# Other PSUM banks for a late group, a merge moved to the end, and five unread matmuls in a spectral-mixing kernel

## The reference

```python
xf = jnp.fft.rfft2(x, axes=(1, 2), norm='ortho')
o1r = relu(xr @ w1[0] - xi @ w1[1] + b1[0])
o1i = relu(xi @ w1[0] + xr @ w1[1] + b1[1])
o2r = softshrink(o1r @ w2[0] - o1i @ w2[1] + b2[0], 0.01)
o2i = softshrink(o1i @ w2[0] + o1r @ w2[1] + b2[1], 0.01)
out = jnp.fft.irfft2(o2r + 1j * o2i, s=(H, W), norm='ortho') + x
```

## Time and profile before

| what | value |
|---|---|
| median of 3 runs | 5476.74 us (5476.72 to 5477.54) |
| the profiled execution's own time | 5478.67 us |
| its span, first to last instruction | 5475.4 us |
| PE busy, share of the span | 97% |
| DVE busy | 67% |
| ACT busy | 41% |
| mean granted TensorE clock | 0.993 |

### The profile page before, as it was taken

How to read it: one execution, slowest core, us unless ns; L and a number is a source line. 1 busy time by engine, 2 the same in 40 slices (tenths; PEclk the granted TensorE clock), 3 DMA queues, 4 the chain that set the end, 5 groups by cost and what they waited for, 6 DMA issues and landing times.

```text
span 5475.4 us, 112300 instructions
## 1 busy us (share of the span) xinstructions
PE 5302.9 (97%) x44352; PEld 4309.3 (79%) x44352; DVE 3684.5 (67%) x5859; ACT 2217.8 (41%) x3457; POOL 627.1 (11%) x420
## 2 busy tenths in 40 slices
PE   6999999999999999999999999999999999999998
PEld 5777887778777787777877777787778877787777
DVE  5676676676666766767667676676666766766665
ACT  3443434434344343444433443334434344343442
POOL 0110011110111101111011110011100111101111
PEclk9999999999999999999999999999999999999999
DMA  3331333312333113331133321333312333123311
GB/s 101 94 84 29 84 94 94 96 30 70 94 94 98 44 54 94 94 98 48 51 94 94 98 65 35 92 94 98 79 38 75 94 98 94 37 62 94 98 48 47
DMA packets 1065693, 421.12 MB, mean 77 GB/s; under 512 B 1062816, under 2 KB 1062944, under 8 KB 1065120
## 3 DMA queue, kind: packets, MB, share of 16 engines
q1 hardware_dynamic: 1060384, 411.62, 28.2%
q10 hardware_dynamic: 4736, 1.60, 0.1%
HBM read 210.26 MB, written 201.33 MB: 75 GB/s over the span
## 4 chain that ended last, share of the span: by engine, by line
issue 89%; POOL 11%; POOLq 0%; DVE 0%
POOL x L774 11%; POOLq L773 0%; POOLq L777 0%; DVE x L726 0%; POOLq L774 0%; POOLq L786 0%
## 5 line engine op out<-in xcount | busy, mean ns | idle before, releaser
L774 POOL TENSOR_TENSOR x<-shrink_or_v,x 128x480 f32<-128x480 f32 (+1 forms) x416 | 626.9, 1507 | 4840.6 <-DVE shrink_or_v L719 4800.9
L691 DVE TENSOR_TENSOR shrink_or_v<-ps,wts 128x768 f32<-128x768 f32 (+1 forms) x544 | 502.0, 923 | 993.1 <-PE ps L478 993.1
L478 PE MATMUL ps<-wts,hbig 128*128 128x192 f32 x4160 | 821.6, 340 | 0.0
L399 PE MATMUL ps<-tab,ring_h 128*128 128x128 f32 x6144 | 726.7, 283 | 46.2 <-DVE ring_h L745 46.2
L399 PEld LDWEIGHTS ps<-tab,ring_h 128*128 128x128 f32 x6144 | 720.6, 199 | 55.6 <-DVE ring_h L745 55.6
L478 PEld LDWEIGHTS ps<-wts,hbig 128*128 128x128 f32 x4160 | 661.0, 189 | 122.2 <-issue 122.2
L572 ACT COPY zbig<-ps 128x512 f32<-128x512 f32 (+1 forms) x544 | 309.1, 568 | 966.5 <-PE ps L415 966.5
L580 ACT ACTIVATE hsmall<-ps,wts 128x256 f32<-128x256 f32 (+1 forms) x544 | 254.6, 468 | 1084.8 <-PE ps L451 1084.8
L386 PE MATMUL ps<-tab,ring_a 128*64 128x128 f32 x6144 | 680.5, 273 | 3.8 <-ACT ring_a L541 3.8
L387 PE MATMUL ps<-tab,ring_a 128*63 128x128 f32 x6144 | 680.4, 273 | 0.0
L386 PEld LDWEIGHTS ps<-tab,ring_a 128*64 128x64 f32 x6144 | 671.3, 137 | 8.3 <-ACT ring_a L541 4.7
(11 more groups left out here) (52 smaller groups left out, 6620.3 us busy)
## 6 DMA issues: line engine op xcount, KB each, us to landing
x<-in_x SPq DMA_DIRECT2D x128, 1536.0 KB, 12.4
out<-x SPq DMA_DIRECT2D x352, 480.0 KB, 4.8
out<-x SPq DMA_DIRECT2D x32, 432.0 KB, 4.1
wts<-in_mix SPq DMA_DIRECT2D x16, 513.0 KB, 3.6
out<-x SPq DMA_DIRECT2D x32, 240.0 KB, 4.2
out<-x SPq DMA_DIRECT2D x32, 192.0 KB, 4.3
ydg<-row ACTq DMA_DIRECT2D x32, 48.0 KB
yedge<-row ACTq DMA_DIRECT2D x32, 0.8 KB
```

Source lines behind the costliest of these rows:

```text
L399: mm = pe.matmul(ps[:, line_bank(1, g), j * 128:(j + 1) * 128], ring_h[g % RING_H][:, j, :], mat("inv_h"), start=True, stop=True)
L478: mm = pe.matmul(o, hbig[u % 2][:, k * H:(k + 1) * H], mix_part("w2_big"), start=False, stop=True, skip_group_check=True)
L691: dve.tensor_tensor(parts(v), d, b2, ALU.add).then_inc(bias_done, 1)
L774: pool.tensor_tensor(xs[p][:, a:b, :], ucopy[g % 4][:, 0:b - a, :], mirror(xs[p], a, b), ALU.add).then_inc(plus_ready, 1)
```

## The change

1. The second layer of group 15 goes to banks 0 and 1 and no longer to 5 and 6. It waits until ACT and DVE have copied the last transforms out of banks 0 and 1 (`zbig_ready`, `zsmall_ready`) and no longer until DVE has added the bias of group 14.
2. Group 16's second layer goes to bank 5 and waits for the bias of group 14. The merge goes to bank 7.
3. `merge` stands behind the second layer of group 16.
4. Five matmuls of 128 x 128 x 128, which nothing reads, are written to bank 6: two where the merge stood and three behind it (`keep_warm`).
5. ACT packs the first tile before the relu of group 16 and the second right behind it (`early_pack`). Then follow the copy of the merged edges and the other four tiles. Each `early_pack` waits for `shrunk` of group 14.

```diff
-        ZBIG_BANK, ZSMALL_BANK, BIG_BANK, SMALL_BANK, OUT_BANK, LAST_BANK = 0, 1, 2, 4, 5, 7
-        E_BANK = ZSMALL_BANK
+        ZBIG_BANK, ZSMALL_BANK, BIG_BANK, SMALL_BANK, OUT_BANK, E_BANK = 0, 1, 2, 4, 5, 7
...
+        def out_banks(u):
+            bank = ZBIG_BANK if u == NU - 2 else OUT_BANK
+            return slice(bank, bank + 2)
...
                 def mix2_rows(q, u):
                     pe.wait_ge(hid_ready, NU * q + u + 1)
-                    if 0 < u < NU - 1:
-                        pe.wait_ge(bias_done, NU * q + u)
+                    if u == NU - 2:
+                        pe.wait_ge(zbig_ready, NU * (q + 1))
+                        pe.wait_ge(zsmall_ready, NU * (q + 1))
+                    elif u:
+                        pe.wait_ge(bias_done, NU * q + min(u, NU - 2))
...
+                def keep_warm(q, n):
+                    pe.wait_ge(bias_done, NU * q + NU - 2)
+                    for i in range(n):
+                        pe.matmul(ps[:, OUT_BANK + 1, 0:H], mat("inv_h"), mat("fwd_h"), start=True, stop=True)
...
                         mix1_rows(q, NU - 1)
-                        merge(q)
+                        keep_warm(q, 2)
                         mix2_rows(q, NU - 1)
                         mix2_whole(q, NU - 1)
+                        merge(q)
+                        keep_warm(q, 3)
                         inverse_lines(q)
...
+                def early_pack(q, g):
+                    act.wait_ge(shrunk, NU * q + NU - 2)
+                    act.copy(*pack_moves(g, LATE, 128)).then_inc(packed_act, 1)
...
+                            if it == NU:
+                                early_pack(q, 0)
                             if it >= 1:
                                 relu(q, it - 1)
...
+                        early_pack(q, 1)
                         act.wait_ge(merge_done, q + 1)
                         act.copy(ydg[:, 0:2, :].rearrange("p k c -> p (k c)"),
                                  ps[:, E_BANK, 0:2 * CB]).then_inc(merged, 1)
-                        act.wait_ge(shrunk, NU * q + NU - 2)
-                        for g in range(RING_H):
-                            act.copy(*pack_moves(g, LATE, 128)).then_inc(packed_act, 1)
+                        for g in range(2, RING_H):
+                            early_pack(q, g)
```

More of the change, by code:

```diff
@@ L306, in big_cols, with out_bank @@
             return (len(evens(u)) + len(odds(u))) * H
-        def out_bank(u):
-            return LAST_BANK if u == NU - 1 else OUT_BANK
+        def out_banks(u):
+            bank = ZBIG_BANK if u == NU - 2 else OUT_BANK
+            return slice(bank, bank + 2)
+        def out_bank(u, i):
+            return range(8)[out_banks(u)][i]
         def small_rows(u):
@@ L469, in mix2_rows @@
                             half = slice(i * SMALL, (i + 1) * SMALL)
-                            pe.matmul(ps[:, out_bank(u) + i, k * 2 * CB:(k + 1) * 2 * CB],
+                            pe.matmul(ps[:, out_bank(u, i), k * 2 * CB:(k + 1) * 2 * CB],
                                       hsmall[u % 2][half, k * H:(k + 1) * H],
@@ L476, in mix2_whole @@
                     for k in range(n + len(odds(u))):
-                        o = ps[:, out_bank(u) + k // n, k % n * 2 * CB:(k % n + 1) * 2 * CB]
+                        o = ps[:, out_bank(u, k // n), k % n * 2 * CB:(k % n + 1) * 2 * CB]
                         mm = pe.matmul(o, hbig[u % 2][:, k * H:(k + 1) * H], mix_part("w2_big"),
@@ L682, in parts @@
                         return t.rearrange("p (i k c) -> p i k c", i=halves, c=2 * CB)
-                    d = ps[:, out_bank(u):out_bank(u) + halves, 0:ne * 2 * CB].rearrange("p i (k c) -> p i k c", c=2 * CB)
+                    d = ps[:, out_banks(u), 0:ne * 2 * CB][:, 0:halves].rearrange("p i (k c) -> p i k c", c=2 * CB)
                     b2 = mix_part("b2").rearrange("p (i k c) -> p i k c", i=1, k=1).broadcast_to([128, halves, ne, 2 * CB])
```

## The result

| | before | changed |
|---|---|---|
| median | 5476.73 us (5473.81 to 5477.54, 4 runs) | 5402.85 us (5402.58 to 5403.81, 4 runs) |
| profiled execution, its own time | 5478.67 us | 5402.93 us |
| span | 5475.4 us | 5400.7 us |
| mean granted clock | 0.993 | 0.999 |

The changed kernel takes 0.9866 of the time before, 95% interval 0.9849 to 0.9883. The forecast was 5401 us, range 5391 to 5424.

What follows compares the result with a forecast made beforehand. PE, busy 97% of the span, bounds the kernel through work, idle time and lowered clock. 43.2 us of path plus 32.6 us of falls off 5478.67 us gives 5402.9; the median lies 1.9 lower: 5401 us, range 5391 to 5424.

Steps and rivals of the forecast that it cites:

- The sum: Whole kernel: 43.2 us from 32 shorter steps plus 32.6 us of clock falls, 75.8 us, giving 5402.9 us profiled.
- The first wait goes: Group 15's second layer no longer waits for group 14's bias and starts 1.30 us earlier in each step.
- Who is late next: ACT's relu, behind a pack, sets the start of group 16's second layer, 1.35 us earlier (1.30 to 1.39).
- the sign that the prediction named: In the profile after, group 16's second layer idles about 0.35 us behind two unread matmuls, waiting for ACT's relu.
- rival C: Pack ahead of group 16's relu costs nothing: 1.58 us a step, 5393.5 us; chance 0.76, shared with forecast and another rival.
- The chain behind it: From group 16's second layer to the inverse lines still 2.55 us; merge and four packs hidden, about 0.15 us idle.
- The unread matmuls cost nothing: All five hide in PE's waits at the end of mixing; with nothing hiding them, 1.13 us a step, 36 us.
- All falls go: All 20 clock falls at inverse-line starts vanish as PE's idle stretches shrink: 1.63 us each, 32.6 us at most.
- What takes them away: Unread matmuls fill PE's idle stretches at the end of mixing; without them 0.8 us each would remain.

Runs made afterwards that it cites:

- run 7: The changed kernel without the two unread matmuls ahead of group 16's second layer, keeping the three behind the merge: 5398.3 us.
- Run 6: The changed kernel with ACT's first early pack moved from ahead of group 16's relu to behind it: 5403.4 us.
- fill_only: The kernel before with five unread matmuls added in PE's wait ahead of the inverse lines, nothing else changed: 5444.0 us.
- fill_first: The kernel before with five unread matmuls between the second layers of groups 14 and 15, the later wait left idle: 5473.6 us.
- last_two: The changed kernel with only two unread matmuls, both behind the merge, and none ahead of group 16's second layer: 5398.5 us.
- no_fill: The changed kernel without its five unread matmuls, everything else kept: 5411.7 us, ratio 0.9881.
- last_three: The same run as run 7: the changed kernel with only the three unread matmuls behind the merge: 5398.3 us.
- banks_only: The changed kernel with the merge back between group 16's layers, no unread matmuls and all packs behind the merged copy: 5412.1 us.
- row0_early: The changed kernel with the next step's first matmul moved behind the merge, two unread matmuls after it, no other filler: 5392.6 us.
- banks_longer: The kernel of banks_only with five unread matmuls added mid-mixing at group 8, lengthening the step and touching neither wait: 5475.7 us.
- last_three_longer: The kernel of last_three with five more unread matmuls in the middle of the mixing, where PE is never idle: 5436.2 us.

## Why the prediction was right

It was right in time, in sign and in both of its sources. Not every step of it held, and part of the closeness is luck. The sum gave 5402.9 us for the profiled execution, which took 5402.93 us. But the path brought 45.1 us and not 43.2, the falls 32.2 us and not 32.6, and the turns of the loop, which the sum does not have, took 2.5 us back.

- **The first wait goes.** Right, with a size off: 1.20 us, not 1.30. L484 to L476 takes 1.50 us, where I had taken the 1.40 us to L442 for the successor. In the changed kernel too L445 comes 1.40 us after L484 (2167.96 against 2166.56), so L476 (64*128 in the trace) starts 0.10 us later behind L484 than L445 (128*128) does. Why is not shown.
- **Who is late next.** L476 of group 16 is 1.42 us earlier (forecast 1.35). ACT's relu sets it where the two unread matmuls are left out (0.49 us of idle PE in runs 1 and 7). In the changed kernel the two unread matmuls reach up to it and hold it themselves: the sign that the prediction named, about 0.35 us of idle time before this L476, did not come, and the waits list none. The size given for the relu was wrong too. I had the pack ahead hold the small part of the relu and the big part follow it by 0.36 us. The big part followed by 0.26 us, and it also has to wait for L462. This was there to be read before: L583 started at 2199.96, just after PE's L459 ended at 2199.92:

```profile
2199.44 0.48 PE L459 MATMUL ps<-zsmall,wts 64*128 64x128 f32 x2
```

The step left out this second input. With the relu bound by it and a first wait of 1.30 us, the forecast would have been rival C's 1.58 us. The first wait brought 0.10 us less, and PE took the work up 0.05 us later than I had it, which leaves 1.43 us. That the forecast's 1.35 us lies near the 1.42 us is luck: two errors of about 0.1 us nearly cancelled.

- **Rival C** (5393.5 us if the pack costs nothing) was priced on the same mistake. Run 6 has its condition (the pack is out of the relu's way) and gives 5403.4 us.
- **The chain behind it.** 2.56 us from L476 to L402, forecast 2.55. The merge and the four packs stayed hidden, and the idle time ahead of L402 is 0.13 us (forecast 0.15).
- **The unread matmuls cost nothing.** Nearly: 0.09 us a step, 2.9 us by the steps and 4.5 us by the medians of run 7, for the first two. The trace of the changed kernel shows it too: L476 starts 0.14 us after the relu and not 0.05. The forecast 0.35 us of idle time behind 0.45 us of filler was not there.
- **All falls go.** Right, but the prediction counted both idle stretches, and only the one ahead of the inverse lines matters: fill_only leaves the first and has no fall, fill_first covers it and has 19. Waits of 1.44 us are followed by falls at 20 of 32 starts, and covering them down to 0.33 us takes all 20 away (fill_only). In the changed kernel 0.13 us are left there, and last_two shows no fall with 0.35 us either.
- **What takes them away.** Here the prediction credited the unread matmuls alone, and that was not so. The banks alone left 4 of 20, by shortening the step. The five matmuls account for 8.8 us of the 73.9 when taken out last (no_fill), and for 32.7 us when put in first (fill_only). The two parts overlap, and no split of the 32 us between them is the true one. What the filler adds is that, at the step lengths tried, the result no longer hangs on them.

## What to carry to other kernels

Where the granted clock falls, cover the idle time of PE just ahead of the fall with matmuls into a free bank, and count the falls in the trace. Here two of 128 x 128 x 128 inside a wait of 0.79 us were enough. Do not judge it by the time of one version, because another step length changes the falls as well (4 of 32 at 167.02 us, 19 at 168.14 us). Let filler end before the wait does: the three that ended 0.13 us before it cost nothing by the step (166.73 us in no_fill and last_three), and the two that ran on past the end of the relu cost 0.09 us a step. Better is work that is read, such as the next step's first matmul. When an instruction has several inputs, price each one before saying which holds it.

## What the runs showed of the hardware

**How many starts are hit changes with the length of the step.** With 1.44 us of idle time ahead of the inverse lines, 20, 19 and 19 of 32 starts were hit at steps of 168.23, 168.23 and 168.14 us, and 4 at 167.02 us. With at most 0.35 us left there, none at 166.55, 166.73, 166.74, 166.82, 167.54, 167.85 or 168.23 us; the last of these (fill_only) still had 1.14 us of idle time 7 us earlier. In one program the same idle time is followed by a fall at some starts and not at others (20 and 12 before), and how many are hit changes with the step. What picks the starts is not shown. Stretches of 0.5 us before L476 and 0.8 us before L402 lie between, with 8 falls at a step of 166.73 us and 2 at 167.85 us.

**The turn of the loop.** PE's loop holds two steps. In the changed kernel the first matmul of a turn starts late at 14 of 15 turns, by 0.28 to 0.50 us, 5.5 us in all. Before, it was late at 7 turns, 3.0 us in all. The timeline of the changed kernel at a late turn:

```profile
2047.41 0.97 PE L508 MATMUL ps<-ydg,tab 128*128 128x480 f32 x2
...
2048.57 0.30 PEld L373 LDWEIGHTS ps<-x,tab 128*128 128x128 f32 x2 [0.97 <-issue]
2048.57 0.46 PE L373 MATMUL ps<-x,tab 128*128 128x96 f32 x2 [0.20 <-DVE shrink_or_v L740]
```

and inside the loop body:

```profile
2214.69 0.97 PE L508 MATMUL ps<-ydg,tab 128*128 128x480 f32 x2
...
2215.49 0.36 PE L373 MATMUL ps<-x,tab 128*128 128x96 f32 x2
```

1.16 us at the turn against 0.80. "issue" says that the weight load (PEld) waited for nothing that the profile shows. DVE's L740, named as releaser of the matmul, had ended at 2048.32. Which versions are hit is not explained: none of 15 turns in fill_only, 1 in banks_only, 7 in last_three, 14 in row0_early, all 15 in banks_longer and last_three_longer. No run tests a cause, and it stays open.
